# Scan inputs of a decoder layer: weights held and channels streamed in two column halves, then added and turned by a twofold identity

## The reference, cut to what matters

```python
xz = x @ W_in.T                                   # x: 4 batches x 512 tokens x 256
x_proj, z = jnp.split(xz, 2, axis=-1)             # 512 channels each
x_conv = _silu(conv_b + sum((xp[:, k:k + l, :] * conv_w[:, k] for k in range(4))))
x_dbl = x_conv @ W_xproj.T                        # 512 channels -> 33 numbers a token
Bmat, Cmat = x_dbl[..., :16], x_dbl[..., 16:32]
dt = jnp.clip(jax.nn.softplus(x_dbl[..., -1]), 0.001, 0.1)
```

## Time and profile before

| | us |
|---|---|
| median of 3 runs | 710.21 (709.97 to 711.47) |
| the profiled execution | 709.6 |
| its span in the trace | 708.2 |
| PE busy | 619.1 (87%) |
| DVE busy | 403.2 (57%) |
| ACT busy | 236.3 (33%) |
| POOL busy | 282.1 (40%) |
| mean granted TensorE clock, share of full | 0.925 |

### The profile page before, as it was taken

The page is one execution under the profiler, slowest core; times in us unless marked ns, Lnnn a source line. Parts: engine busy times, 40 slices in busy tenths (PEclk is TensorE's granted clock), DMA queues, the critical chain, the costliest instruction groups (busy, mean ns, idle before and its releaser), DMA issues.

```text
span 708.2 us, 13714 instructions
## 1 busy us (share of the span) xinstructions
PE 619.1 (87%) x3843; PEld 495.4 (70%) x3844; DVE 403.2 (57%) x1207; ACT 236.3 (33%) x467; POOL 282.1 (40%) x195
## 2 busy tenths in 40 slices
PE   5999999798698975486999999999999999999940
PEld 2655659586366654365888888888888888888830
DVE  2566488865748769864545545545445455445524
ACT  3544550002776451223223242241422422322204
POOL 7000010011354446667513838348382274751112
PEclk9999999999899787566999999999999999999975
DMA  8999308104000033222511161512516115111116
GB/s 291 313 335 337 105 1 216 25 1 178 1 1 2 30 128 150 104 100 61 198 30 28 30 208 30 195 30 50 185 30 208 25 22 205 30 30 31 28 23 233
DMA packets 53429, 74.81 MB, mean 106 GB/s; under 512 B 13328, under 2 KB 49552, under 8 KB 52112
## 3 DMA queue, kind: packets, MB, share of 16 engines
q1 hardware_dynamic: 41056, 60.18, 25.6%
q0 software_dynamic: 6864, 9.11, 7.4%
q10 hardware_dynamic: 5472, 5.06, 2.7%
HBM read 42.67 MB, written 31.67 MB: 105 GB/s over the span
## 4 chain that ended last, share of the span: by engine, by line
PE 68%; DVE 15%; POOL 5%; ACT 5%; issue 3%; DMA 3%; POOLq 0%; ACTq 0%; DVEq 0%; SPq 0%
PE bank L2146 27%; PE bank L2166 12%; PE bank L1727 7%; PE bank L1877 4%; PE bank L2156 4%; POOL experts_w L796 3%; PE bank L1737 2%; DVE region L1230 2%; DVE region L1228 1%; DVE small L1247 1%; PE bank L2026 1%; PE bank L2132 1%; ACT region L1103 1%; PE bank L1982 1%; PE bank L2045 1%
## 5 line engine op out<-in xcount | busy, mean ns | idle before, releaser
L2146 PE MATMUL bank<-experts_w,experts_x 128*128 x864 | 218.7, 402 | 3.6 <-POOL experts_w L796 2.3
L2146 PEld LDWEIGHTS bank<-experts_w,experts_x 128*128 128x128 f32 x864 | 158.7, 190 | 37.6 <-issue 4.5
L1659 DVE TENSOR_TENSOR region<-region,bank 128x512 f32<-128x512 f32 x72 | 49.5, 688 | 165.0 <-ACT region L1054 165.0
L1054 ACT ACTIVATE region<-bank 128x512 f32<-128x512 f32 x72 | 43.0, 597 | 244.7 <-PE bank L2146 244.7
L809 POOL DMA_INDIRECT total<-region,rid x36 | 55.7, 1548 | 171.5 <-DVE region L1673 123.9
L2166 PE MATMUL bank<-experts_w 128*128 x864 | 121.1, 290 | 2.1 <-DVE experts_w L1663 2.1
L2166 PEld LDWEIGHTS bank<-experts_w 128*128 128x128 f32 x864 | 107.9, 191 | 2.5 <-issue 2.3
L796 POOL TENSOR_TENSOR experts_w<-wstage,experts_w 128x3072 f32 x12 | 83.4, 6948 | 0.5
L677 POOL TENSOR_TENSOR small<-small 128x4 f32<-128x4 f32 (+4 forms) x18 | 24.6, 1371 | 106.3 <-DVE small L1239 85.6
L1727 PE MATMUL bank<-xcol,region 128*128 128x512 f32 x128 | 57.9, 610 | 8.9 <-DMA xcol<-in_xT 7.3
L1126 DVE SCALAR_TENSOR_TENSOR region<-bank,convw,region 128x511 f32<-128x511 f32 (+2 forms) x48 | 35.9, 749 | 39.1 <-ACT region L852 37.2
(11 more groups left out here) (333 smaller groups left out, 894.3 us busy)
## 6 DMA issues: line engine op xcount, KB each, us to landing
wstage<-in_w_exp SPq DMA_DIRECT2D x8, 3072.0 KB, 10.7
slots<-padrow SPq DMA_DIRECT2D x8, 2210.0 KB, 19.8
region<-slots ACTq DMA_DIRECT2D x38, 130.0 KB, 2.1
xcol<-in_xT SPq DMA_DIRECT2D x4, 512.0 KB, 7.3
xtok<-in_x SPq DMA_DIRECT2D x1, 2048.0 KB, 12.8
region<-in_ctxT SPq DMA_DIRECT2D x1, 2048.0 KB, 7.9
region<-in_ctx SPq DMA_DIRECT2D x4, 512.0 KB, 9.0
region<-total SPq DMA_DIRECT2D x4, 512.0 KB, 5.5
```

Source lines behind the costliest of these rows:

```text
L1054: act.activation(gsil[:, u], bank[2 * u][:, :], ACT.Silu).then_inc(sil_done, 1)
L1659: dve.tensor_tensor(hmid[:, u], gsil[:, u], bank[2 * u + 1][:, :], ALU.mult).then_inc(mid_done, 1)
L2146: mm = pe.matmul(bank[2 * u + m][:, :], (xTh, xTl)[a][:, s, k, :], moving(off, w, m * KD * F + k * F + u * HALF, HALF), start=(k == 0 and ...
```

## The change

`scan_inputs(b)` now has the weights of the projection held in the array: for each channel group j one matmul with the 33 columns of `wxT[:, j]`, padded with zeros to 64, as weights, and all 512 tokens of `xc` streaming. Even groups write partitions 0 to 63 of bank 4, odd groups partitions 64 to 127, so that two groups use the two halves of the array's columns. Each half sums its two groups. The result, item `("xdT", b)`, has scan inputs on partitions and tokens along the free dimension; ACT copies it to `xdT`. Four matmuls then take 128 tokens of `xdT` as weights and stream `twofold`, a matrix of 33 columns with ones at rows n and n + 64: it adds the two halves and turns tokens onto partitions. That is `("xd", b)` as before. The 16 transposes are split, eight between the projection and these four matmuls, eight after. `wxT` moved into `yx` and has 64 columns a group, and POOL clears the padding and builds `twofold`.

```diff
+        xdT = ybuf(0, 0)
+        wxT = ybuf(0, 1)[:, 0:NJ * P // 2].rearrange("p (j n) -> p j n", j=NJ)
+        twofold = ybuf(0, 2)[:, 0:NX]
...
+        def plan_inputs(b):
+            plan(("xdT", b), 4)
+            plan(("xd", b), 4)
+            for q in range(NQ):
+                plan(("xt", NQ * b + q), 5 + (NQ * b + q) % 3)
...
-            sp.dma_start(wxT, w_xT.rearrange("(j p) n -> p j n", p=P)).then_inc(ld_conv, 16)
+            sp.dma_start(wxT[:, :, 0:NX], w_xT.rearrange("(j p) n -> p j n", p=P)).then_inc(ld_conv, 16)
...
+            link(pool.memset(wxT[:, :, NX:], 0.0))
+            link(pool.tensor_tensor(twofold, ident[:, 0:NX], ident[:, P // 2:P // 2 + NX], ALU.add))
...
+            def input_sums(b):
+                wait_filled(act, ("xdT", b))
+                if b:
+                    wait_filled(act, ("xd", b - 1))
+                drain(("xdT", b), act.copy(xdT, ps(("xdT", b))[:, :]))
...
                 if n % NJ == 2 and n > NJ:
+                    input_sums(n // NJ - 1)
                     by_tokens(n // NJ - 1)
...
+            input_sums(B - 1)
             act.wait_ge(ld_small, 16 * 6)
...
             def scan_inputs(b):
-                o = claim(("xd", b))
+                o = claim(("xdT", b))
                 for j in range(NJ):
                     pe.wait_ge(xc_done, NJ * b + j + 1)
-                    for q in range(NQ):
-                        t = b * S + q * P
-                        mm = pe.matmul(o[:, q * NX:(q + 1) * NX], xc[:, j, t:t + P], wxT[:, j, :],
-                                       start=(j + q == 0), stop=(j == NJ - 1 and q == NQ - 1))
-                fill(("xd", b), mm)
-                for q in range(NQ):
+                    half = slice(64 * (j % 2), 64 * (j % 2) + 64)
+                    mm = pe.matmul(o[half, :], wxT[:, j, :], xc[:, j, b * S:(b + 1) * S], start=(j < 2), stop=(j >= NJ - 2))
+                fill(("xdT", b), mm)
+
+                def by_tokens(q):
                     i = NQ * b + q
                     o = claim(("xt", i))
                     for j in range(NJ):
                         mm = pe.transpose(o[:, j * P:(j + 1) * P], xc[:, j, i * P:(i + 1) * P], ident[:, :])
                     fill(("xt", i), mm)
+                for q in range(2):
+                    by_tokens(q)
+                o = claim(("xd", b))
+                for q in range(NQ):
+                    mm = pe.matmul(o[:, q * NX:(q + 1) * NX], xdT[:, q * P:(q + 1) * P], twofold, start=True, stop=True)
+                fill(("xd", b), mm)
+                for q in range(2, NQ):
+                    by_tokens(q)
```

More of the change, by code:

```diff
@@ L190, in decoder_kernel @@
         woutT = sb("woutT", NJ * D)[:, :].rearrange("p (j d) -> p j d", j=NJ)
-        wxT = sb("wxT", NJ * NX)[:, :].rearrange("p (j n) -> p j n", j=NJ)
         convw = sb("convw", NJ * TAPS)[:, :].rearrange("p (j k) -> p j k", j=NJ)
@@ L327, in decoder_kernel @@
                 b = n // NJ - 1
-                plan(("xd", b), 4)
-                for q in range(NQ):
-                    plan(("xt", NQ * b + q), 5 + (NQ * b + q) % 3)
+                plan_inputs(b)
         for n in range(GATES_LAST, B * NJ):
             plan(("z", n), 2 + n % 2)
-        plan(("xd", B - 1), 4)
-        for q in range(NQ):
-            plan(("xt", NQ * (B - 1) + q), 5 + (NQ * (B - 1) + q) % 3)
+        plan_inputs(B - 1)
         for n, k in (("cumB", 1), ("cumC", 2), ("cumD", 3), ("cumA", 0), ("abT", 4), ("vbT", 5), (("S", 0), 6), (("S", 1), 7),
```

## The result

| | before | after |
|---|---|---|
| median, us | 710.45 (709.96 to 711.52, 6 runs) | 706.31 (705.28 to 708.16, 6 runs) |
| ratio of the times | | 0.9953 (0.9933 to 0.9973) |
| profiled execution, us | 709.6 | 707.8 |
| its span, us | 708.2 | 706.3 |

The change made the kernel faster, by 4.1 us in the medians and by 3.3 us (1.9 to 4.8) in the ratio. The forecast was 706.7. A second measurement gave 706.55 (12 runs) against 710.42 (23 runs), ratio 0.9955 (0.9935 to 0.9975).

The account below looks back on a forecast made before the run. PE was taken to bound the first stage, with a clock drop in batch 1. Batches 0 to 2 gain 2.10 us, batch 3 loses 0.19, the clock gives 1.62: 3.5 us, from 710.2 to 706.7, range 704.9 to 710.1.

Parts of the forecast that it names:

- The bound: First stage: PE works end to end, so its savings in scan inputs 0 to 2 count in full.
- The break on DVE: DVE's release of a bank at 66.1 us: comes earlier by as much as PE is earlier.
- The projection with held weights: Four matmuls, eight records a batch: column halves overlap, four rounds of 0.43, 1.72 us.
- slower rival: Projection: the pairs do not overlap, 3.44 us instead of 1.72, 713.6 us in all; chance 0.09.
- The rule on weight loads: Projection: halves sharing rows would pay a load each round, 2.2 us, 708.6 in all; kept as rival, chance 0.05.
- The change of form: PE switching between full array and halves, in and out: 0.10 us each, 0.20 a batch.
- The copy: ACT's copy of xdT, 1.98 to 2.58 us into the block, hidden by eight transposes; uncovered, some tenths a batch.
- Batch 3: Last scan inputs: x_dbl ready after 3.69 us instead of 3.50, 0.19 later.
- Start of the program: POOL's two more operations and the wxT load: taken as 0, bounds 0 and 0.3 us.
- The clock: Batch 1's scan inputs: the drop of the granted clock goes, 1.62 us gained; bound 0.
- The rival of the later stage: Later stage: two more clock drops, or drops at PE's dense work, take all: about 710.0 us; chance 0.12.
- the rival with one drop coming back: A clock drop of 1.6 us stays or returns, leaving 1.9 us gained: 708.3; chance 0.24.

Follow-up runs that it names:

- one_half: The changed kernel with all four channel groups in the lower column half: 716.08 us against 713.03 for the kernel before, ratio 1.0053.
- no_cover: The changed kernel with the twofold matmuls straight behind the projection, all sixteen transposes after them: 708.36 us, ratio 0.9982 to the kernel before.
- interleaved: The kernel before, narrow matmuls of batches 0 to 2 in four groups, each followed by four transposes: 705.46 us (ratio 0.9951), then 708.55 (0.9962).

## Why the prediction was right

**The bound.** PE end to end in the first stage, and a lead there carried to the end: shown by two pairs of profiles with like clocks, 3.6 us at x_dbl and 3.5 at the end in one, 3.8 and 3.9 in the other. The break on DVE moved with PE, as forecast: from the end of PE's work before it to PE's next projection it took 8.43 us before (57.74 to 66.17) and 8.43 after (55.50 to 63.93).

**The projection with held weights.** 1.72 us of stream in four rounds; the chain gives 1.87 with the way back to the full array, and one_half gives 3.58 for the same records in one half. The prediction read the overlap from L1807 and L1982, and that is what the chip did. Its slower rival gave 8.7 - 4x for the gain of the first stage without the clock; between the two forms x grew by 1.71, for which that is 6.8 us; between the medians 7.5 were measured, and the 0.7 lie within the intervals of the two measurements.

**The rule on weight loads.** The two halves share all rows. Eight records with eight loads, of 0.13 to 0.14 us each, took 1.87 us on the chain, of which four rounds of stream are 1.72: no load is exposed. The Trainium skill says in "TensorE: Matmul & The Clock Gate", Part 3 (Packing small matmuls), that weight loads overlap running matmuls only if the row group differs. The trace does not agree, and the measurement decides, for column halves. Nor did the loads show where a single half took all eight records: 8 x 0.43 = 3.44 us of stream, 3.58 measured.

**The change of form.** 0.20 a block was taken, in and out. The block on the chain is 4.61 where the prediction's terms with the transposes make 0.20 + 1.72 + 0.87 + 1.80 = 4.59. So a block saves 0.68 us, not 0.70.

**The copy.** Forecast 1.98 to 2.58 us into the block, measured 1.99 to 2.58. The cover was worth 0.82 a block, as no_cover showed; the prediction had said some tenths.

**Batch 3.** Forecast 0.19 us later. From the start of the block on the chain to DVE's copy it was 3.59 before (87.34 - 83.75) and 3.82 after (84.64 - 80.82): 0.23.

**Start of the program.** Forecast nothing. With the rise of the clock at 12.39 us the changed kernel reaches its first block at 30.68 on the chain, and so does the kernel before with the rise at 12.48.

**The clock.** 1.62 us for a drop that goes. The profiles bear it out for batch 1 (three of three before, none in the two of the changed kernel), with 1.6 us each, and the interleaved kernel shows that the unbroken narrow stretch is what it hangs on. The prediction had one profile to go by and could not know that its drop stands there each time; that it does was luck. It missed that a second drop could come at batch 3, which was in two profiles of three and moved x_dbl by another 0.3 to 0.4 us.

**Sum.** 3.5 us forecast; the blocks give 3 x 0.68 - 0.23 + 1.63 = 3.44, and both profiles of the changed kernel 3.45 up to x_dbl. At the end it was 3.5 and 3.9 in the pairs, 3.3 and 3.2 by the ratios of the two measurements, 4.1 and 3.9 in their medians. The rival of the later stage is real as scatter: the first profile of the changed kernel lost 1.8 us in the out-projection against the first profile before, and two of the three profiles before have that same loss. The ratios alone could not tell the forecast from the rival with one drop coming back (1.9 us, at the edge of both intervals); the pairs of profiles do.

What stays open: why a drop comes at batches 1 and 3 of the unbroken order and not at 0 and 2; and why one execution in a few runs 4 us under the rest (706 against 710 us in the kernel before, 8 of 35 runs on one chip). The two profiles of interleaved put such a difference into routing and attention, where the granted clock differed; what decides it between executions was not tried.

## What to carry to other kernels

A matmul that streams few columns past a full load of weights costs its load, not its stream: 0.109 us a record for 33 columns here, where a transpose with 128 columns took 0.113, and weight loads filled 5.25 of the block's 5.30 us. If the narrow side has at most 64 columns, hold it as weights and stream the long side in two column halves; this pays only with the halves side by side (1.87 against 3.58 us), and the turning back must be hidden behind work that does not need it. When a stretch of PE work is fully busy but runs slow, look at the granted clock of the window behind it: breaking a long run of narrow matmuls with other work was enough here, with all of its matmuls kept.

## What the runs showed of the hardware that was not expected

- The two column halves do not need an alternating order. With both matmuls of the lower half issued ahead of both of the upper half, the eight records took 1.87 us as before.
- A busy PE can lose its clock: 2.8 to 3.6 us after the start of a block with an unbroken stretch of matmuls of 33 columns, PE never idle, the granted clock fell to 0.50 for 3.4 us, in 6 of 15 such blocks (batch 1 in all three profiles of the kernel before). The same instructions in pieces of 0.81 us between transposes kept it at 1.00 in six blocks of six.
- Narrow matmuls in pieces are also slightly cheaper by themselves: 5.13 us a block instead of 5.29 at full clock.
- The moment at which the clock first rises is not tied to the program. It was at 10.92, 12.48 and 12.14 us in three profiles of the kernel before, and PE's first scan-input record lay between 29.6 and 30.6 us in those and in the two of the changed kernel, which have the same work ahead of it. Two profiles can differ by 1 us for this alone, so leads should be read between executions with like clocks.
